# A local transformer's inverse norms on GpSimd, with copied queries and keys, and the feed-forward's first norm inside the attention's last turns

## The reference, cut to what matters

```python
h = shift_token(x)
q, k, v = split(h @ wqkv)                       # 8 heads of 64
l2norm = lambda t: t / jnp.clip(jnp.linalg.norm(t, axis=-1, keepdims=True), 1e-12)
q, k = l2norm(q) * qs, l2norm(k) * ksc
q, k = rotary_xpos(q, k)                        # t * cos * scale + rotate_half(t) * sin * scale
o = local_attention(q, k, v)                    # windows of 128, each sees itself and the one before
x = x + o @ wo
h = shift_token(x)
h = (h - h.mean(-1)) / jnp.sqrt(h.var(-1) + 1e-05) * lg + lb
a, g = split(h @ w1 + b1)
x = x + (a * gelu(g)) @ w2 + b2
```

## Time and profile before

| what | value |
|---|---|
| median of 3 runs | 3231.86 us (3226.63 to 3234.86) |
| the profiled execution's own time | 3224.11 us |
| its span, first to last instruction | 3222.0 us |
| TensorE busy in the span | 2949.9 us (92%) |
| VectorE busy | 2207.8 us (69%) |
| ScalarE busy | 1978.7 us (61%) |
| GpSimd busy | 218.6 us (7%) |
| mean granted TensorE clock | 0.974 |
| the first layer's attention | about 2427 to 2699 us |
| the second layer's attention | about 2822 to 3092 us |

### The profile page before, as it was taken

The page is one execution under the profiler, slowest core; times in us unless marked ns, Lnnn a source line. Parts: engine busy times, 40 slices in busy tenths (PEclk is TensorE's granted clock), DMA queues, the critical chain, the costliest instruction groups (busy, mean ns, idle before and its releaser), DMA issues. The chain is left out here.

```text
span 3222.0 us, 70760 instructions
## 1 busy us (share of the span) xinstructions
PE 2949.9 (92%) x29314; PEld 1465.9 (45%) x29314; DVE 2207.8 (69%) x2752; ACT 1978.7 (61%) x2682; POOL 218.6 (7%) x325
## 2 busy tenths in 40 slices
PE   6999999999999999999999896999986887978878
PEld 3444444444444444444444563222234664656655
DVE  6888788888888888888788855000027775677756
ACT  5665655655656656556556424999975774267732
POOL 0000000000000000000000101100003323043200
PEclk8999999999999999999999898999998998999989
DMA  2000000000000000000000003111101001000000
GB/s 78 7 2 2 8 2 8 2 2 8 2 2 8 2 2 8 2 4 2 2 3 2 31 1 128 27 27 36 27 13 49 20 1 58 1 17 17 1 1 27
DMA packets 30032, 51.64 MB, mean 16 GB/s; under 512 B 6071, under 2 KB 22538, under 8 KB 28554
## 3 DMA queue, kind: packets, MB, share of 16 engines
q1 hardware_dynamic: 29706, 46.91, 4.7%
HBM read 41.04 MB, written 5.83 MB: 15 GB/s over the span
## 5 line engine op out<-in xcount | busy, mean ns | idle before, releaser
L734 ACT ACTIVATE a_probs<-PS 128x1024 f32<-128x1024 f32 x928 | 949.6, 1024 | 602.7 <-PE PS L489 599.5
L502 PE MATMUL PS<-a_probs,a_V 64*64 64x512 f32 x7424 | 980.0, 590 | 5.6 <-DVE a_heads_outT L915 4.6
L956 DVE TENSOR_TENSOR a_prob_sums<-a_prob_sums,a_probs 128x1024 f32<-128x1024 f32 x512 | 627.4, 1225 | 153.4 <-ACT a_probs L734 137.7
L953 DVE SCALAR_TENSOR_TENSOR a_prob_sums<-a_probs,a_valid,a_prob_sums 128x1024 f32<-128x1024 f32 x384 | 481.1, 1253 | 70.4 <-ACT a_probs L734 60.3
L489 PE MATMUL PS<-a_Q_hi,a_K_hi 64*64 64x512 f16 x3712 | 385.0, 381 | 5.5 <-ACT a_probs L734 4.7
L1772 ACT ACTIVATE c_probs<-PS 128x1024 f32<-128x1024 f32 (+1 forms) x416 | 382.9, 1080 | 8.4 <-PE PS L1691 6.6
L489 PE MATMUL PS<-a_Q_lo,a_K_hi 64*64 64x512 f16 x3712 | 384.0, 377 | 1.2 <-issue 1.1
L489 PE MATMUL PS<-a_Q_hi,a_K_lo 64*64 64x512 f16 x3712 | 382.1, 377 | 1.8 <-issue 1.8
L502 PEld LDWEIGHTS PS<-a_probs,a_V 64*64 64x64 f32 x7424 | 290.1, 133 | 165.6 <-issue 21.1
L489 PEld LDWEIGHTS PS<-a_Q_hi,a_K_hi 64*64 64x64 f16 x3712 | 119.0, 106 | 275.7 <-issue 270.4
L489 PEld LDWEIGHTS PS<-a_Q_hi,a_K_lo 64*64 64x64 f16 x3712 | 119.5, 107 | 228.0 <-issue 224.3
(11 more groups left out here) (325 smaller groups left out, 4177.6 us busy)
## 6 DMA issues: line engine op xcount, KB each, us to landing
c_Qop<-q_part SPq DMA_DIRECT2D x96, 64.0 KB, 2.2
c_Kop<-k_part SPq DMA_DIRECT2D x96, 50.0 KB, 2.0
d_raw<-in_l1f_w_dram SPq DMA_DIRECT2D x18, 256.0 KB, 3.2
d_tables<-in_rotary_dram SPq DMA_DIRECT2D x2, 2048.0 KB, 10.8
X<-in_x_dram SPq DMA_DIRECT2D x2, 1024.0 KB, 9.5
out_dram<-X SPq DMA_DIRECT2D x4, 512.0 KB, 3.5
c_cT<-in_ctxT_dram SPq DMA_DIRECT2D x1, 1601.0 KB, 6.6
a_probs<-in_ctx_dram SPq DMA_DIRECT2D x3, 512.0 KB, 5.0
```

Source lines behind the costliest of these rows:

```text
L502: last = nc.tensor.matmul(m.PS[64 * h:64 * h + 64, PVB + g, :], V[e][rows, s, 64 * h:64 * h + 64], probs[n % 4][rows, h * BANK:(h + 1) * B ...
L734: nc.scalar.activation(probs[n % 4][:], m.PS[:, b0:b0 + 2, :].rearrange("p b c -> p (b c)"), ACT.Exp).then_inc(exped, 1)
L953: nc.vector.scalar_tensor_tensor(out=sums, in0=new, scalar=valid[:, s:s + 1], in1=sums, op0=ALU.mult, op1=ALU.add).then_inc(summed, 1)
L956: nc.vector.tensor_tensor(sums, sums, new, ALU.add).then_inc(summed, 1)
```

## The change

Three things are done.

1. The inverse norms of windows 3 to 15 are computed on GpSimd, from the sums of squares: clip at the squared limit, the power of -0.5, and one correction step, in six instructions of 128x16 that each wait for the one before. Windows 0 to 2 keep ScalarE's root and VectorE's maximum and reciprocal. ScalarE copies projected queries and keys from PSUM to SBUF (`keep`, L2130 of the new kernel), `make_unit` reads that copy, and the projections' bank is free after `keep` rather than after `make_unit`.
2. Orders change. ScalarE: `move_spread(w)` at the end of turn w rather than at the start of the next; `square` ahead of `move_input`; the tables of windows 0 to 2 loaded explicitly. VectorE: `make_unit` behind the maxima and `add`, `invert` ahead of `straighten`, `sum_squares` ahead of `rotate`. TensorE: `apply` in two halves with `spread` between them.
3. The feed-forward's first norm moves into the attention's last turns (a class `ShiftedNorm` holds its functions and tiles, used by both blocks): in turn 13 the shifts of chunks 0 and 1, in turn 14 the statistics and root of chunk 0, in turn 15 `stage(0)`, `statistics(1)`, `turn_h(0)` and `move_h(0)`, and after the last turn `split_h(0)`. The feed-forward begins with `raise_tiles(0)`, and with `root(1)` and `stage(1)` on the other engines.

```diff
@@ TensorE
-                def apply(w):
+                def apply(w, g):
...
-                    for c in range(4):
-                        if c % 2 == 0:
-                            after(pe, "probs_moved", 2 * (base + w) + c // 2 + 1)
+                    after(pe, "probs_moved", 2 * (base + w) + g + 1)
+                    for c in (2 * g, 2 * g + 1):
...
+                    if w == ST - 3:
+                        tn.shift_half(pe, l, 0)
+                        tn.shift_half(pe, l, 1)
+                    if w == ST - 1:
+                        tn.turn_h(pe, l, 0)
                     if inside(w + 1):
                         turn(w + 1)
...
                         for g in range(2):
                             turn_probs(w, g)
+                        apply(w, 0)
                         spread(w)
-                        apply(w)
+                        apply(w, 1)
@@ ScalarE
+                def keep(w):
+
+                    after(act, "squared", base + w + 1)
+                    after(act, "united", base + w)
+                    nc.scalar.activation(kept[:].rearrange("p h d -> p (h d)"),
+                                         m.PS[:, qk_bank(w):qk_bank(w) + 2, :].rearrange("p b c -> p (b c)"),
+                                         ACT.Copy).then_inc(s["kept"], 1)
...
-                        root(w + 3)
+                        keep(w + 3)
+                    if w == ST - 3:
+                        tn.move_shifted(act, l, 0)
+                        tn.move_shifted(act, l, 1)
+                    if w == ST - 2:
+                        tn.root(act, l, 0)
+                        nc.scalar.preload_act_table(ACT.Exp)
+                    if w == ST - 1:
+                        tn.move_h(act, l, 0)
@@ VectorE
+                    dve.wait_ge(s["kept"], base + w + 1)
                     after(dve, "crossed", base + w - 1)
                     nc.vector.tensor_tensor(
-                        unit[w % 2][:].rearrange("p q h a d -> p (q h) (a d)"),
-                        m.PS[:, qk_bank(w):qk_bank(w) + 2, :].rearrange("p b (h d) -> p (b h) d", d=LD),
-                        norms[:, 3, :].unsqueeze(2).to_broadcast([P, 16, LD]), ALU.mult).then_inc(s["united"], 1)
+                        unit[w % 2][:].rearrange("p q h a d -> p (q h) (a d)"), kept[:],
+                        norms[:, 4, :].unsqueeze(2).to_broadcast([P, 16, LD]), ALU.mult).then_inc(s["united"], 1)
...
+                    if w == ST - 2:
+                        tn.statistics(dve, l, 0)
+                    if w == ST - 1:
+                        tn.stage(dve, l, 0)
+                        tn.statistics(dve, l, 1)
+                tn.split_h(dve, l, 0)
@@ GpSimd
+                    squared, first, product, step, inverse_root, limited = (norms[:, i, :] for i in range(6))
...
+                    nc.gpsimd.tensor_scalar(limited, squared, SQUARE_CLIP, None, ALU.max).then_inc(s["norm_step"], 1)
+                    pool.wait_ge(s["norm_step"], steps + 1)
+                    nc.gpsimd.tensor_tensor(first, limited, minus_half[:], ALU.pow).then_inc(s["norm_step"], 1)
+                    pool.wait_ge(s["norm_step"], steps + 2)
+                    nc.gpsimd.tensor_tensor(product, limited, first, ALU.mult).then_inc(s["norm_step"], 1)
+                    pool.wait_ge(s["norm_step"], steps + 3)
+                    nc.gpsimd.tensor_tensor(step, product, first, ALU.mult).then_inc(s["norm_step"], 1)
+                    pool.wait_ge(s["norm_step"], steps + 4)
+                    nc.gpsimd.tensor_scalar(product, step, -0.5, 1.5, ALU.mult, ALU.add).then_inc(s["norm_step"], 1)
+                    pool.wait_ge(s["norm_step"], steps + 5)
+                    nc.gpsimd.tensor_tensor(inverse_root, product, first, ALU.mult).then_inc(s["rooted"], 1)
```

294 lines of the change are left out of this document (160 added, 134 removed).

## The result

| | before | after |
|---|---|---|
| time, median (lowest to highest, 4 runs each) | 3229.24 us (3225.94 to 3234.86) | 3205.11 us (3202.98 to 3205.41) |
| ratio, 95% interval | | 0.9927 [0.9913, 0.9941] |
| the profiled execution: time, span | 3224.11, 3222.0 us | 3205.41, 3203.6 us |

The changed kernel is faster by 0.73%, or 24.1 us by the medians. By the two profiled executions it is 18.7: the execution of before that was profiled lay 5 us under its median, that of after on it. What follows explains the 18.4 us between the spans.

A forecast was written before the change was run, and what follows sets the result against it. Bound: a chain across engines, no engine saturated. 1.4 + 9.8 + 1.1 + 4.0 = 16.3 a layer, 32.6 for two, from the profiled 3224.1 to 3191.5; with 7.8 to the median, forecast 3199, range 3183 to 3222.

The forecast's parts named there:

- The bound: Full attention turn: a chain between engines; the mask waits 1.54 beyond the scores for table load, root and make_unit.
- make_unit ... goes behind the maxima: 0.21: VectorE's turn: make_unit runs from 0.21 to 1.44 after the second exponentials' start.
- the forecast 14.65: Steady attention turn: 14.65 instead of 15.40, a gain of 0.75 a turn, 9.8 a layer over thirteen turns.
- The collisions: VectorE and GpSimd together: straighten 1.83, cross 3.74, expand or rotate loses up to 0.7; steady loss 0.3 a turn.
- its turn of 15.0 to 15.2: Second rival, chance 0.17: VectorE-GpSimd collisions paid in full, gain 0.2 a turn, 6.0 a layer, kernel 3220.
- spread between the halves of apply, 0.48: TensorE's turn: spread between apply's halves starts the scores at 8.27 instead of 7.79, costing 0.48.
- GpSimd's root, "about 2": GpSimd's six instructions on 128x16 take about 2 us and hide before the next make_unit.
- keep at nothing: End of ScalarE's turn: the PSUM copy of 1.03 costs nothing, covered by idle time before the next exponentials.
- The prologue: Before turn 0's first mask: make_unit(2) goes behind it, three keeps give some back; gain 1.4, bounds 0.4 and 2.1.
- Turns 13 and 14: Shift matmuls fill TensorE's gap in turn 13, gain 1.1 (0 to 1.6); turn 14 keeps its gap, nothing.
- Turn 15 and the norm: Attention's end: first raising matmul 18.8 after the last exponentials instead of 22.86; gain 4.0, bounds 2.5 and 4.5.
- The FFN is bound by TensorE and doesn't notice: Feed-forward: earlier stage(1), chunk 1's square root and Gelu table load change nothing; no gain counted.

The follow-up runs named there:

- experiment on this order: Changed kernel with make_unit(w+2) ahead of add(w-1) on VectorE, not behind it: 3188.88 us, ratio to before 0.9889.
- the experiment on GpSimd's queue in the feed-forward: Changed kernel with GpSimd's copy for chunk 2's norm ahead of splitting the next layer's weights: 3197.06 us, ratio to before 0.9914.
- the experiment on it: Changed kernel with turn_h(0) on TensorE behind window 15's last apply, not ahead of its probabilities' transposes: 3196.3 us, ratio to before 0.9908.
- both with expand between the halves: GpSimd's expand between cross's halves: on the changed kernel 3191.06 us; on the kernel with three kept edits and spread ahead of apply 3160.19 us.
- the one with half of cross: Changed kernel with the keys' half of GpSimd's cross left out from window 3 on: 3192.0 us, ratio to before 0.9887.

## Why the prediction was right and wrong

Direction and range held; 3205.1 came where 3199 was forecast. But the profiled span fell by 18.4 where the sum had 32.6, and the median looks nearer only because I added the 7.8 between profiled execution and median, which the changed kernel does not have.

- **The bound: right.** Table load, root and scaling were late in the turn. With the scaling out of the mask's way, the mask waits for the scores, by its row above. With the roots back on ScalarE it still does: what the loads cost before hung on the scaling's place ahead of the mask.
- **"make_unit ... goes behind the maxima: 0.21": wrong, and the step that failed.** I set it directly behind the maxima. In VectorE's queue the addition to Z stands between them, and that waits 0.41 for TensorE's `mix`, which the scores of this very turn delay. Measured 0.71. I had counted this wait only as one of TensorE's ("about 1 are waits for make_unit and add"), not as one on VectorE with make_unit queued behind it. The experiment on this order gives back 0.5 a turn, that is 13 to 16 us, as much as the turns had fallen short. That its turns then lie at the forecast 14.65 is in part luck: it has no wait for `expanded`, where I had 0.3, and 0.2 more in the handovers around spread.
- **The collisions: mechanism right, sizes off.** Straighten was to take 1.83 and takes 2.20; cross 3.74 and takes 3.70. The loss of `expand`, priced at "up to 0.7", is 1.00: its copies (0.74 alone) and rotate (1.23 alone) together took 1.74, not far under their sum of 1.97. There the rule of the Trainium skill (page "SBUF — State Buffer", section "Who interferes with whom"), that the two engines block each other for the whole instruction, is nearer to the trace than my row from the prologue, and its turn of 15.0 to 15.2 is what came. It isn't the whole reason, though: in the experiment on the order cross collides as much as before, and the turn is 14.6. `expanded` was expected at 7.1 and is there at 7.4.
- **spread between the halves of apply, 0.48: too small.** From apply's start to the scores it is 3.21, with spread's wait of 0.50 in it: 2.71 against the 2.42 I had used, 0.3 more over three handovers.
- **GpSimd's root, "about 2": wrong by more than two**, since one instruction, the power, takes 2.93. It was hidden, as forecast, but with 2.3 us of room and not 3.7.
- **keep at nothing, TensorE doesn't take over, no table load in the steady turn: right.** ScalarE waits 3.10 for the maxima, where I had said about 4.
- **The prologue: 0.5 and 0.8 for 1.4**; it wasn't taken apart further, and lies within its bounds. **Turns 13 and 14: 1.7 and -0.1 for 1.1.** In turn 13 TensorE's gap is filled and the sixteen transposes take 1.94, where they had taken 3.64 and 3.55; this turn gains 0.9 and 0.4. In turn 14 the gap stays (4.46 idle), and there the layers part: 15.38 in the first, 16.58 in the second. The granted clock behind the gap was 0.50 over all of the second layer's transposes (3.6 us) and into `apply`, and 0.67 over the first layer's. The kernel of the experiment on GpSimd's queue in the feed-forward, with the same code here, has 15.38 in both. So the 1.2 are put down to the clock that this execution met; why it met it stays open.
- **Turn 15 and the norm: 5.3 and 4.4 for 4.0**, each step found in its place and 1.2 earlier, as the staging came at 3.96 and not 4.9. turn_h ahead of the probabilities cost what was reckoned, and the experiment on it shows it.
- **"The FFN is bound by TensorE and doesn't notice": wrong in the first layer**, where TensorE waits 2.47 for chunk 2. Matmuls that start earlier meet a split of weights on GpSimd that doesn't, by the experiment on its queue. This wait ate what the full clock at the start gave (96.7 from the first raising matmul to the last idle time, 97.0 before), and the clock of 0.50 in the block's last stretch made the loss of 1.7. In the second layer, which has no weights to split, the feed-forward gained 2.2. Most of it is the warm start that I hadn't counted (1.9 by my estimate): from the first raising matmul to the last idle time it takes 94.03 in the three kernels that begin there at 1.00, and 95.3 to 95.7 in the eight others with this norm.

## What to carry to other kernels

When an instruction is moved along a queue, write down all that stands ahead of it in its new place with each one's own wait; here half a microsecond of someone else's wait cost two thirds of what the turns were to gain, and exchanging two calls brought it back. This loop had other chains close behind it: an edit that took 1.8 us out of it gained only the distance to the next (0.5), so edits are to be priced against the second-longest path too. A small instruction ahead of one that others wait for can cost more than a large one in a wait: two of 0.17 and 0.25 us on VectorE cost 0.35 a turn, two table loads of 1.28 nothing. And when an edit brings work forward, look for what it leaves behind: transfers that land no earlier, and what is queued behind whoever waits for them.

## What the hardware showed that was not expected

- GpSimd's power on 128x16 took 2.93 us (26 of them, 76.2 in all), where its multiplications of the same size took 0.22 and its tensor-scalar operation 0.20 to 0.25. At the same tile size the power took thirteen times as long as the multiplication.
- The same GpSimd work costs by its neighbour: expand's two copies 0.73, 1.20, 1.67 or 1.74; four products of cross 2.77 to 3.75. VectorE beside it pays less in rotate (1.33 for 1.23), and more in straighten (2.20 for 1.29).
- GpSimd's power took 3.32 instead of 2.93 in three kernels (both with expand between the halves, and the one with half of cross), and there in 54 cases of 54 where its first 0.53 us lay beside VectorE's second half of the weights, which has two inputs in SBUF. In the last root of each layer with expand between the halves its first 0.94 lay beside `rotate`, and it took 3.73. In all other cases it took 2.90 to 2.94. So the power lost 0.4 and 0.8 by a neighbour that it ran beside for 0.5 and 0.9.
- Two table loads a turn (2.56 us of ScalarE) cost nothing of the turn once the scaling stood behind the masks: the one delayed a product that the mask didn't wait for, the other lay inside a wait.
- Behind the same idle time the same code met a granted clock of 0.50 in some kernels and not, or for a shorter time, in others, at three places: turn 14 of the second layer (1.2 us), the last stretch of the first layer's feed-forward (1.7) and that of the second's (1.7). There is one profile of each kernel, so whether a kernel keeps to one of them from execution to execution isn't known. Of single profiles, differences of this size are no sign of an edit.
